# Opening of a macaron transformer block: statistics merge, low-part product and fill-in products rearranged

## The chip, the cores and the metric

The kernel runs on one core of one Trainium2 chip. The metric is device time in microseconds (us) of one execution; the median of the runs is given.

## What is computed

The input x is (4, 1024, 128) in float32. Three sub-layers follow each other: half of a mixture-of-experts feed-forward, an attention without softmax, and the same feed-forward again, each behind a layer norm and added to x. Cut to what matters here:

```python
def ffn(x):                                   # E = 16 experts, 2 shared units, F = 128
    scores = sigmoid(x @ router_w.T)          # group-limited top-4 of scores + bias
    combine = ...                             # (tokens, 16), 2.5 * normalised weights
    h = einsum('td,edf->etf', x, gate_w)
    u = einsum('td,edf->etf', x, up_w)
    y = einsum('etf,efd->etd', silu(h) * u, down_w)
    return einsum('etd,te->td', y, combine) + silu(x @ sh_gate_w) * (x @ sh_up_w) @ sh_down_w
x = x + 0.5 * ffn(layernorm(x))
x = x + attention(layernorm(x))
x = x + 0.5 * ffn(layernorm(x))
```

All 18 units (2 shared, 16 routed) are computed for every token; the combine weights are zero where an expert was not chosen.

## The kernel before

The 4096 tokens are eight blocks of 512. One **step** is one block through one feed-forward, so there are 16 steps, and a step has 18 **units** of 512 tokens each. A Python loop `pair(p, ...)` on every engine writes out two steps (36 units, `u` from 0 to 35, `w = u % 18`); only the first pair, where `first` is true, matters here, and its first step is the code's `early`. In the text, step 0, 1 and 2 are the first, second and third step, and unit u is that of step 0.

A float32 product is made of three products of rounded operands (`product`, L447): high weights by high activations (L449), low weights by high activations (L450), high weights by low activations (L451). A unit is nine such 128x512 products on TensorE: gate, up, and the down product of the unit four before it (`LAG = 4`). Around them:

- ScalarE: silu of the gate (L840), `A_hi`, the rounded product (L814), `W_hi`, the rounded weights (L718), copies of the transposed next block `XT` (L743) and its rounding `XT_hi` (L747), and the normalised next block `XN` (L733).
- VectorE: silu by combine weight `T` (L1137), that by up `A` (L1168), the routing of the next step in eight parts (`route`, L958 on), and the statistics of the step after: `bn_stats` (L938) and their merge (`merge_stats`, L899 to L912, called by `stats`).
- GpSimd: low parts, which are the difference of a value and its rounding: `W_lo` of the weights (L333), `A_lo` of the products (L340), `XT_lo` of the next block (`next_low`, L359), and the power -0.5 of the variance (L351).
- SyncE's queue issues every transfer.

Each engine's order is the order of the code; engines meet at semaphores. In step 0 the weights come in and are split while the first units run, so GpSimd has a `W_lo` beside most `A_lo` (table `SPLIT_AT`: units 4, 5 and 7 to 12).

Places that the change touches. At the start TensorE does 13 fill-in products (`keep_busy(WARM)`), a transpose, 2 fill-ins, four transposes of block 0 into the PSUM bank `prepP` (L480), the router logits (L488), and then `first_units` (L578 on), whose first gate product waits for `XT_lo` of step 0. The four transposes of `comb` at L569 (`spread`), behind the gate of unit 4, wait for the whole routing of step 0. PSUM bank `prepP` holds in turn the transposed block, the logits of the next step and the scratch tiles of `route`. The statistics of step 1 are merged in the prologue with one operand or the result of each instruction in PSUM (L1213 to L1227); those of step 2 are merged behind unit 13 by `merge_stats`, with all operands in SBUF. TensorE's gate of unit u waits for `T` of unit u - 2 (`gate_left`).

Of the kernel before, what the change touches and what calls it, by code (L numbers as in the profile page):

```python
# [28 lines left out]
F32 = mybir.dt.float32  # L29
F32R = mybir.dt.float32r  # L30
ALU = mybir.AluOpType
ACT = mybir.ActivationFunctionType
AX = mybir.AxisListType

P = 128
HEAD = 4
EPS = 1e-5
GROUPS, PER_GROUP = 4, 4
# [4 lines left out]
TILES = BLOCK // P  # L43
# [5 lines left out]
def macaron_kernel(nc, x, Wqkv_w, Wqkv_b, gn_w, gn_b, out_w, out_b, router_w, bias,  # L49
                   gate_w, up_w, down_w, sh_gate_w, sh_up_w, sh_down_w, out):  # L50
    BATCH, SEQ, D = x.shape
    E = router_w.shape[0]
# [14 lines left out]
    WARM, FILL = 13, 2  # L67
# [12 lines left out]
    with ctx:  # L80
# [15 lines left out]
        XT_hi = sb("XT_hi", [P, 2, BLOCK], F32R)  # L96
        XT_lo = sb("XT_lo", [P, 2, BLOCK], F32R)
# [8 lines left out]
        bst = sb("bst", [P, TILES, 6])  # L106
# [85 lines left out]
        prepP = pb("prepP")  # L192
# [136 lines left out]
        def _(pool):  # L329
# [61 lines left out]
            def pair(p, first, attention, last):  # L391
                n = PAIR * p
                for u in range(PAIR):
                    w, s = u % UNITS, u // UNITS
                    early = first and s == 0
                    if early and u in SPLIT_AT:
                        split_low(SPLIT_AT[u])
                    if first and u == 24:
                        pool.memset(XA[:, :, :], 1.0)
                    if w == 14 and not last:  # L400
                        step_rstd(2 * p + s + 2)
                    if w == (7 if early else 2) and not (last and s == 1):
                        next_low(2 * p + s + 1, (s + 1) % 2)
                    if attention and u == 4:

                        pool.wait_ge(att_seq, ATT_OPS * (p - ATT0) + 6)
                        pool.tensor_tensor(arstd[:, :], avar[:, :], half[:, :],
                                           ALU.pow).then_inc(att_pow, 1)
                        pool.wait_ge(att_pow, 3 * (p - ATT0) + 1)
                        pool.tensor_tensor(ashift[:, :], anmean[:, :], arstd[:, :],  # L410
                                           ALU.mult).then_inc(att_pow, 1)
                    if attention and u == 28:

                        pool.wait_ge(att_seq, ATT_OPS * (p - ATT0) + 17)
                        pool.tensor_tensor(grstd[:, :], gvar[:, :], half[:, 0:1],
                                           ALU.pow).then_inc(att_pow, 1)
                    if not (first and u == 0):
                        split_activations(n + u - 1, (u - 1) % SLOTS)
                    if attention and u in (33, 34):
                        g = u - 33  # L420
                        if g == 0:

                            pool.wait_ge(att_seq, ATT_OPS * (p - ATT0 + 1))
                        xb = X[:, bass.ds((p - ATT0) * BT + g * TILES, TILES), :]
                        pool.tensor_tensor(xb, xb, brow[:, :].unsqueeze(1).broadcast_to([P, TILES, P]),
                                           ALU.add).then_inc(row_added, 1)
# [17 lines left out]

        @block.tensor
        def _(pe):
            def product(dst, hi_w, lo_w, hi_x, lo_x, start, stop):  # L447

                pe.matmul(dst, hi_w, hi_x, start=start, stop=False)  # L449
                pe.matmul(dst, lo_w, hi_x, start=False, stop=False)  # L450
                return pe.matmul(dst, hi_w, lo_x, start=False, stop=stop)  # L451

            def down(n, u, t):
# [29 lines left out]
            def logits(t):  # L483

                pe.wait_ge(xt_ready, t + 1)
                bank = backP if isinstance(t, int) and t == 0 else prepP
                for j in range(TILES):
                    mm = pe.matmul(bank[:, j * E:(j + 1) * E], XT[:, j * P:(j + 1) * P], RT[:, :],  # L488
                                   start=True, stop=True)
                mm.then_inc(logits_done, 1)  # L490
# [87 lines left out]
            def first_units():  # L578

                def one(dst, u, i):  # L580
                    return product(dst[:, :], W_hi[:, u, i, :], W_lo[:, u, i, :], XT_hi[:, 0, :],
                                   XT_lo[:, 0, :], True, True)

                def gate(u):
                    pe.wait_ge(w_lo_done, u + 1)
                    if u == 0:
                        pe.wait_ge(xt_lo_ready, 1)
                    if u >= 2:
                        pe.wait_ge(silu_done, u - 1)
                    one(gateP[u % 2], u, 0).then_inc(gate_done, 1)  # L590

                def up(u):
                    one(first_up[u], u, 1).then_inc(up_done, 1)

                gate(0)
                up(0)
                gate(1)
                up(1)
                gate(2)
                gate(3)  # L600
                up(2)
                up(3)
                gate(4)
                pe.wait_ge(route_seq, ROUTE_OPS)
                spread(0)
                spread(1)
                transpose_weights(0)
                gate(5)

                pe.wait_ge(ct_ready, 1)  # L610
                up(4)
                pe.wait_ge(mul_done, 2)
                up(5)

                pe.wait_ge(gate_weighted, 1)
                spread(2)
                pe.wait_ge(mul_done, 3)
                spread(3)
                gate(6)

                pe.wait_ge(mul_done, 4)
                down(0, 0, 0)
                transpose_next(1)
                down(0, 1, 0)
# [65 lines left out]
            pe.transpose(attP[:, 3 * P:3 * P + E], R_in[:, :], ident[0:E, 0:E]).then_inc(setup_psum, 1)  # L690
            keep_busy(FILL)
            transpose_next(0)
            pe.wait_ge(setup_sb, 1)
            logits(0)
            pair(0, True, False, False)
# [202 lines left out]
        def _(dve):  # L898
# [37 lines left out]
            def rows(t, blk):  # L936
# [2 lines left out]
                                       .rearrange("p o d -> p (o d)"))  # L939
                ins.then_inc(stats_seq, 1)  # L940

            def stats(t):
                merge_stats(stats_seq, 4 * t, bst, nmean[:, :], vareps[:, :], parts)

# [10 lines left out]
            gscp = scratch(6, GROUPS)  # L955
            grank = prepP[:, TILES * (7 * E + GROUPS):TILES * (7 * E + 2 * GROUPS)]
            wsump = prepP[:, TILES * (7 * E + 2 * GROUPS):TILES * (7 * E + 2 * GROUPS + 1)]

            def route(t, part):
                base = ROUTE_OPS * t  # L960
# [1 line left out]
                selp4 = selp.rearrange("p t (g i) -> p (t g) i", i=PER_GROUP)  # L962
                if part == 0:
                    dve.wait_ge(logits_done, t + 1)
                    flat = (backP if isinstance(t, int) and t == 0 else prepP)[:, 0:TILES * E]

                    near_f = near[:, :, :].rearrange("p t e -> p (t e)")

# [171 lines left out]
            def pair(p, first, attention, last):  # L1140
                n, t0 = PAIR * p, 2 * p
                for u in range(PAIR):
# [27 lines left out]
                    if w == 13 and not (first and s == 0):  # L1170
                        residual(t0 + s - 1, 2 * ((p - 1 + s) % BATCH) + (1 - s))
                    if not (last and s == 1):
                        at = 6 if early else 0
                        if at + 2 <= w < at + 10:
                            route(t0 + s + 1, w - at - 2)
# [6 lines left out]
                        dve.wait_ge(mul_done, n + u + 1)  # L1182
                        rows(t0 + s + 2, 2 * ((p + 1) % BATCH) + s)
                    if w == (13 if early else 12) and not last:
                        stats(t0 + s + 2)
                    if first and u == PAIR - 1:
                        dve.tensor_scalar(blkm[:, :], blk1[:, :], 1.0 / HEAD, None,
                                          ALU.mult).then_inc(attended, 2)
# [98 lines left out]
```

## Time and profile before

| | |
|---|---|
| median of 3 runs | 670.13 us (669.88 to 670.77) |
| the profiled execution's own time | 671.6 us |
| its span, first to last instruction | 669.9 us |
| busy: TensorE, VectorE, GpSimd, ScalarE | 661.1, 522.3, 446.5, 406.4 us |
| mean granted clock of TensorE | 0.995 |

The profile lists instructions by line of the kernel, with out<-in by tile names. A timeline row is start, duration, engine, line, operation, operands, count, and in brackets how long the engine had been idle before it and what released it. TensorE rows overlap, since products are pipelined, so the distance of starts is the cost of one. The granted clock is 1.00 at 2.4 GHz and 0.50 at 1.2 GHz.

### The profile page before, as it was taken

How to read it: one execution, taken by the hardware profiler on the slowest of the kernel's cores; microseconds unless marked ns; L12 is line 12 of the kernel's file. 1: busy time of each engine (PE TensorE's matmuls, PEld its weight loads, DVE VectorE, ACT ScalarE, POOL GpSimd, SP SyncE). 2: the span in 40 equal slices, each digit the busy share in tenths (PEclk: the TensorE clock that was granted, in tenths of full speed). 3: DMA queues.
4: the chain of work that ended last, by engine and by line, in shares of the span. 5: the costliest groups of instructions: out<-in, count | busy, mean ns of one | idle time of the engine just before them, and what ended most of it. 6: DMA issues, size and time to landing. Idle time of an engine off the chain costs nothing.

```text
span 669.9 us, 10547 instructions
## 1 busy us (share of the span) xinstructions
PE 661.1 (99%) x3165; PEld 551.2 (82%) x3165; DVE 522.3 (78%) x1440; ACT 406.4 (61%) x817; POOL 446.5 (67%) x386
## 2 busy tenths in 40 slices
PE   7989999999999999999999999999999999999997
PEld 6868888888888888888888888888888888888886
DVE  6796969778687886878868778687795978868664
ACT  4856565565676556765657656676656565655554
POOL 6996666666756677666676666766667666666663
PEclk8999999999999999999999999999999999999999
DMA  9715170320506015060160510703306033150700
GB/s 232 264 58 201 54 252 2 139 114 27 226 2 234 20 45 211 0 221 33 26 229 1 199 55 17 252 1 134 136 12 259 0 131 139 46 225 0 270 0 32
DMA packets 30262, 75.38 MB, mean 113 GB/s; under 512 B 3569, under 2 KB 12545, under 8 KB 30209
## 3 DMA queue, kind: packets, MB, share of 16 engines
q1 hardware_dynamic: 30208, 74.74, 31.0%
q8 instruction: 25, 0.41, 0.2%
q14 instruction: 29, 0.23, 0.1%
HBM read 72.11 MB, written 2.62 MB: 112 GB/s over the span
## 4 chain that ended last, share of the span: by engine, by line
PE 96%; DVE 1%; DMA 1%; SPq 0%; POOL 0%; issue 0%; ACT 0%; DVEq 0%
PE gateP L449 10%; PE yP L451 10%; PE yP L449 10%; PE gateP L451 10%; PE gateP L450 10%; PE upP L451 10%; PE yP L450 10%; PE upP L449 10%; PE upP L450 10%; PE prepP L488 2%; PE attP L505 1%; PE backP L469 1%; PE prepP L480 1%; DMA W_in<-in_L_ffn_sh_down_w_dram 1%; PE attP L561 1%; PE backP L561 1%
## 5 line engine op out<-in xcount | busy, mean ns | idle before, releaser
L340 POOL TENSOR_TENSOR A_lo<-A,A_hi 128x512 fp32r<-128x512 f32 x287 | 370.6, 1293 | 205.2 <-ACT A_hi L814 205.2
L840 ACT ACTIVATE gateP<-gateP 128x512 f32<-128x512 f32 x252 | 146.6, 582 | 203.6 <-PE gateP L451 202.7
L1137 DVE TENSOR_TENSOR T<-gateP,CB 128x512 f32<-128x512 f32 x252 | 173.3, 688 | 89.1 <-ACT gateP L840 84.8
L814 ACT CAST A_hi<-A 128x512 fp32r<-128x512 f32 x287 | 176.0, 613 | 12.4 <-DVE A L1168 9.5
L1168 DVE TENSOR_TENSOR A<-upP,T 128x512 f32<-128x512 f32 x254 | 175.6, 691 | 8.7
L449 PE MATMUL gateP<-XT_hi,W_hi 128*128 128x512 f32 x288 | 119.1, 414 | 2.1 <-DVE T L1137 1.7
L449 PE MATMUL yP<-A_hi,W_hi 128*128 128x512 f32 x288 | 113.5, 394 | 0.0
L451 PE MATMUL yP<-A_lo,W_hi 128*128 128x512 f32 x288 | 112.9, 392 | 0.0
L451 PE MATMUL gateP<-XT_lo,W_hi 128*128 128x512 f32 x288 | 112.8, 392 | 0.0
L450 PE MATMUL gateP<-XT_hi,W_lo 128*128 128x512 f32 x288 | 112.7, 391 | 0.0
L450 PE MATMUL yP<-A_hi,W_lo 128*128 128x512 f32 x288 | 112.3, 390 | 0.0
L451 PE MATMUL upP<-XT_lo,W_hi 128*128 128x512 f32 (+1 forms) x286 | 112.1, 392 | 0.0
L449 PE MATMUL upP<-XT_hi,W_hi 128*128 128x512 f32 (+1 forms) x286 | 112.1, 392 | 0.0
L450 PE MATMUL upP<-XT_hi,W_lo 128*128 128x512 f32 (+1 forms) x286 | 111.8, 391 | 0.0
L449 PEld LDWEIGHTS yP<-A_hi,W_hi 128*128 128x128 f32 x288 | 54.2, 188 | 13.2 <-POOL A_lo L340 1.9
L451 PEld LDWEIGHTS gateP<-XT_lo,W_hi 128*128 128x128 f32 x288 | 54.3, 189 | 11.8
L449 PEld LDWEIGHTS gateP<-XT_hi,W_hi 128*128 128x128 f32 x288 | 54.7, 190 | 11.2 <-issue 2.1
L451 PEld LDWEIGHTS yP<-A_lo,W_hi 128*128 128x128 f32 x288 | 54.2, 188 | 11.7
L451 PEld LDWEIGHTS upP<-XT_lo,W_hi 128*128 128x128 f32 x286 | 54.1, 189 | 11.7
L450 PEld LDWEIGHTS upP<-XT_hi,W_lo 128*128 128x128 f32 x286 | 54.0, 189 | 11.6
L449 PEld LDWEIGHTS upP<-XT_hi,W_hi 128*128 128x128 f32 x286 | 53.9, 188 | 11.7
L450 PEld LDWEIGHTS yP<-A_hi,W_lo 128*128 128x128 f32 x288 | 54.2, 188 | 11.0
(223 smaller groups left out, 647.0 us busy)
## 6 DMA issues: line engine op xcount, KB each, us to landing
CB<-combT SPq DMA_DIRECT2D x126, 512.0 KB, 6.9
out_dram<-X SPq DMA_DIRECT2D x7, 256.0 KB, 2.0
X<-in_L_attn_x_dram SPq DMA_DIRECT2D x3, 512.0 KB, 9.8
W_in<-in_L_ffn_gate_w_dram SPq DMA_DIRECT2D x4, 256.0 KB, 5.2
W_in<-in_L_ffn_up_w_dram SPq DMA_DIRECT2D x4, 256.0 KB, 5.3
W_in<-in_L_ffn_down_w_dram SPq DMA_DIRECT2D x4, 256.0 KB, 5.4
X<-in_L_attn_x_dram SPq DMA_DIRECT2D x2, 256.0 KB, 3.1
combT<-CT SPq DMA_DIRECT2D x16, 32.0 KB, 1.8
```

The source lines that it names most:

```text
L340: pool.tensor_tensor(A_lo[:, slot, :], A[:, slot, :], A_hi[:, slot, :].bitcast(F32), ALU.subtract).then_inc(low_done, 1)
L449: pe.matmul(dst, hi_w, hi_x, start=start, stop=False)
L450: pe.matmul(dst, lo_w, hi_x, start=False, stop=False)
L451: return pe.matmul(dst, hi_w, lo_x, start=False, stop=stop)
L469: mm = pe.transpose(backP[:, j * P:(j + 1) * P], YT[:, j * P:(j + 1) * P], ident[:, :])
L480: mm = pe.transpose(prepP[:, j * P:(j + 1) * P], XN[:, j, :], ident[:, :])
L488: mm = pe.matmul(bank[:, j * E:(j + 1) * E], XT[:, j * P:(j + 1) * P], RT[:, :], start=True, stop=True)
L561: mm = pe.matmul(bank[:, j * P:(j + 1) * P], XAT[:, g * TILES + j, :], Bm[:, :], start=True, stop=True)
L814: act.copy(A_hi[:, v % SLOTS, :], A[:, v % SLOTS, :]).then_inc(high_done, 1)
L840: act.activation(dst, gateP[u % 2][:, :], ACT.Silu).then_inc(silu_done, 1)
L1137: dve.tensor_tensor(T[:, u % TS, :], silu, weights, ALU.mult).then_inc(gate_weighted, 1)
L1168: dve.tensor_tensor(A[:, u % SLOTS, :], bank[:, :], gated, ALU.mult).then_inc(mul_done, 1)
```

## The change

Four edits, all in the first step or ahead of it:

1. `stats_in_psum` merges the statistics of step 2, behind unit 13 of step 0, in seven instructions, each with an operand or the result in PSUM (free columns of `prepP`), in place of the seven of `merge_stats`.
2. `XT_lo` of step 1 is made on VectorE out of `prepP` behind unit 7, and no longer on GpSimd out of `XT`. So that `prepP` still holds the block, the logits of step 1 go to the bank `backP`.
3. The first gate product of the kernel waits for `XT_hi`, and only its third product for `XT_lo`.
4. Two more fill-in products (`keep_busy(FILL)`) stand between the transposes of block 0 and its logits.

```diff
-                    if w == (7 if early else 2) and not (last and s == 1):
+                    if w == 2 and not early and not (last and s == 1):
                         next_low(2 * p + s + 1, (s + 1) % 2)
...
-            def product(dst, hi_w, lo_w, hi_x, lo_x, start, stop):
+            def product(dst, hi_w, lo_w, hi_x, lo_x, start, stop, low_of_step_0=False):
 
                 pe.matmul(dst, hi_w, hi_x, start=start, stop=False)
                 pe.matmul(dst, lo_w, hi_x, start=False, stop=False)
+                if low_of_step_0:
+                    pe.wait_ge(xt_lo_ready, 1)
                 return pe.matmul(dst, hi_w, lo_x, start=False, stop=stop)
...
-                bank = backP if isinstance(t, int) and t == 0 else prepP
+                bank = backP if isinstance(t, int) and t < 2 else prepP
...
-                        pe.wait_ge(xt_lo_ready, 1)
+                        pe.wait_ge(xt_hi_ready, 1)
...
             transpose_next(0)
+            keep_busy(FILL)
             pe.wait_ge(setup_sb, 1)
             logits(0)
...
+            def stats_in_psum(t, bank, count):
+
+                base = 4 * t
+                sums = bank[:, 0:2 * TILES].rearrange("p (j c) -> p j c", c=2)
+                diffp, within = bank[:, 2 * TILES:3 * TILES], bank[:, 3 * TILES:4 * TILES]
+                both = bst[:, :, :].rearrange("p j (h c) -> p j c h", h=2)[:, :, 1:3, :]
+                dve.wait_ge(stats_seq, base + 1)
+                dve.tensor_reduce(sums, both, AX.X, ALU.add).then_inc(stats_seq, 1)
+                dve.wait_ge(stats_seq, base + 2)
+                for dst in (parts[:, 0, :], diffp):
+                    dve.scalar_tensor_tensor(dst, bst[:, :, 1], 2.0, sums[:, :, 0], ALU.mult, ALU.subtract)
+                dve.tensor_scalar(nmean[:, :], sums[:, :, 0], -0.5, None, ALU.mult)
+                dve.tensor_scalar(within, sums[:, :, 1], 1.0 / P, EPS, ALU.mult, ALU.add).then_inc(stats_seq, 1)
+                dve.wait_ge(stats_seq, base + 3)
+                dve.scalar_tensor_tensor(parts[:, 1, :], parts[:, 0, :], 0.25, diffp, ALU.mult,
+                                         ALU.mult).then_inc(spread_square, 1)
+                dve.wait_ge(spread_square, count)
+                dve.tensor_tensor(vareps[:, :], parts[:, 1, :], within, ALU.add).then_inc(stats_seq, 1)
...
+                        if early and u == 7:
+
+                            dve.wait_ge(xt_hi_ready, 2)
+                            dve.tensor_tensor(XT_lo[:, 1, :], prepP[:, :], XT_hi[:, 1, :].bitcast(F32),
+                                              ALU.subtract).then_inc(xt_lo_ready, 1)
...
-                        stats(t0 + s + 2)
+                        if early:
+                            stats_in_psum(2, prepP[:, FREE_AT:FREE_AT + 4 * TILES], 2)
+                        else:
+                            stats(t0 + s + 2)
```

TensorE's queue at the start, with the semaphores that a row waits for, before:

```order
L480 MATMUL prepP<-ident,XN 128x128 x3
L488 MATMUL backP<-RT,XT 128x16 [waits xt_ready,setup_sb]
L488 MATMUL backP<-RT,XT 128x16 x3
L449 MATMUL gateP<-XT_hi,W_hi 128x512 [waits xt_lo_ready,w_lo_done]
L450 MATMUL gateP<-XT_hi,W_lo 128x512
L451 MATMUL gateP<-XT_lo,W_hi 128x512
```

and now:

```order
L482 MATMUL prepP<-ident,XN 128x128 x3
L578 MATMUL yP<-ones 128x128 x2
L490 MATMUL backP<-RT,XT 128x16 [waits xt_ready,setup_sb]
L490 MATMUL backP<-RT,XT 128x16 x3
L449 MATMUL gateP<-XT_hi,W_hi 128x512 [waits xt_hi_ready,w_lo_done]
L450 MATMUL gateP<-XT_hi,W_lo 128x512
L453 MATMUL gateP<-XT_lo,W_hi 128x512 [waits xt_lo_ready]
```

Two fill-ins stand between the transposes and the logits, and the wait for `XT_lo` has moved two products back.

GpSimd's queue in units 5 to 8 of step 0, before:

```order
L340 TENSOR_TENSOR A_lo<-A,A_hi 128x512 x2
L333 TENSOR_TENSOR W_lo<-W_in,W_hi 128x384
L359 TENSOR_TENSOR XT_lo<-XT,XT_hi 128x512
L340 TENSOR_TENSOR A_lo<-A,A_hi 128x512
L333 TENSOR_TENSOR W_lo<-W_in,W_hi 128x384
```

and VectorE's in units 7 and 8 now (L1160 is `T`, L1191 is `A`, L992 the first instruction of `route` for step 1):

```order
L1160 TENSOR_TENSOR T<-gateP,CB 128x512
L1191 TENSOR_TENSOR A<-upP,T 128x512
L1199 TENSOR_TENSOR XT_lo<-prepP,XT_hi 128x512
L1160 TENSOR_TENSOR T<-gateP,CB 128x512
L1191 TENSOR_TENSOR A<-upP,T 128x512
L992 TENSOR_SCALAR near<-backP 128x64
```

The L359 row is gone from GpSimd's queue in this step, and L1199 stands in VectorE's between `A` of unit 7 and `T` of unit 8.

VectorE's queue behind unit 13 of step 0, before:

```order
L1031 MAX top<-masked 128x8 x4
L903 TENSOR_TENSOR parts<-bst 128x4
L904 TENSOR_TENSOR parts<-bst 128x4
L905 TENSOR_TENSOR parts<-bst 128x4
L907 TENSOR_SCALAR nmean<-parts 128x4
L908 SCALAR_TENSOR_TENSOR parts<-parts 128x4
L909 TENSOR_SCALAR parts<-parts 128x4
L912 TENSOR_TENSOR vareps<-parts 128x4
L1137 TENSOR_TENSOR T<-gateP,CB 128x512
```

and now:

```order
L1054 MAX top<-masked 128x8 x4
L952 TENSOR_REDUCE prepP<-bst 128x8
L955 SCALAR_TENSOR_TENSOR parts<-bst,prepP 128x4
L955 SCALAR_TENSOR_TENSOR prepP<-bst,prepP 128x4
L956 TENSOR_SCALAR nmean<-prepP 128x4
L957 TENSOR_SCALAR prepP<-prepP 128x4
L959 SCALAR_TENSOR_TENSOR parts<-parts,prepP 128x4
L962 TENSOR_TENSOR vareps<-parts,prepP 128x4
L1160 TENSOR_TENSOR T<-gateP,CB 128x512
```

The place and the count of the seven are the same; none has only SBUF operands any more.

## Rows read from the trace of the kernel before

**Rows 1.** The page: TensorE's busy time, and the chain that ended last by engine.

```profile
PE 661.1 (99%) x3165; PEld 551.2 (82%) x3165; DVE 522.3 (78%) x1440; ACT 406.4 (61%) x817; POOL 446.5 (67%) x386
...
PE 96%; DVE 1%; DMA 1%; SPq 0%; POOL 0%; issue 0%; ACT 0%; DVEq 0%
```

**Rows 2.** Windows: busy us by engine, then TensorE's granted clock, DMA share, GB/s.

```profile
10.00:15.00 5.00, 4.66 (x16) 3.66 (x16) 4.48 (x23) 2.72 (x7) 3.65 (x5) 0.66 1.20 292
...
50.00:55.00 5.00, 5.00 (x20) 3.94 (x19) 4.42 (x11) 3.57 (x9) 3.56 (x4) 0.75 0.02 3
```

**Rows 3.** Timeline of TensorE, end of step 0 (start, duration, idle before and releaser).

```profile
36.85 0.46 PE L449 MATMUL yP<-A_hi,W_hi 128*128 128x512 f32 x1
...
45.73 0.50 PE L449 MATMUL yP<-A_hi,W_hi 128*128 128x512 f32 x1
...
46.30 0.39 PE L451 MATMUL yP<-A_lo,W_hi 128*128 128x512 f32 x1
48.41 0.47 PE L449 MATMUL gateP<-XT_hi,W_hi 128*128 128x512 f32 x1 [1.73 <-DVE T L1137]
...
52.60 0.39 PE L451 MATMUL gateP<-XT_lo,W_hi 128*128 128x512 f32 x1
```

**Rows 4.** Timeline of VectorE, units 13 to 15 of step 0.

```profile
43.52 3.42 DVE L903 TENSOR_TENSOR parts<-bst 128x4 f32<-128x4 f32 x1
...
47.58 0.69 DVE L1137 TENSOR_TENSOR T<-gateP,CB 128x512 f32<-128x512 f32 x1
...
49.51 0.68 DVE L1137 TENSOR_TENSOR T<-gateP,CB 128x512 f32<-128x512 f32 x1
```

**Rows 5.** Timeline of GpSimd in step 0.

```profile
31.95 1.33 POOL L359 TENSOR_TENSOR XT_lo<-XT,XT_hi 128x512 fp32r<-128x512 f32 x1
...
41.13 1.07 POOL L333 TENSOR_TENSOR W_lo<-W_in,W_hi 128x384 fp32r<-128x384 f32 x1
...
43.35 1.06 POOL L333 TENSOR_TENSOR W_lo<-W_in,W_hi 128x384 fp32r<-128x384 f32 x1
44.33 2.59 POOL L340 TENSOR_TENSOR A_lo<-A,A_hi 128x512 fp32r<-128x512 f32 x2
47.71 1.01 POOL L351 TENSOR_TENSOR rstd<-vareps,half 128x4 f32<-128x4 f32 x1 [0.80 <-DVE vareps L912]
```

**Rows 6.** Groups of instructions, by form: L903 in the whole kernel (count | busy, mean ns).

```profile
L903 DVE TENSOR_TENSOR parts<-bst 128x4 f32<-128x4 f32 x15 | 7.7, 514 | 0.0
```

**Rows 7.** Timeline of TensorE from the start to the first weights' spread.

```profile
6.44 0.71 PE L576 MATMUL yP<-ones 128*128 128x128 f32 x4
...
9.21 1.03 PE L488 MATMUL backP<-RT,XT 128*128 128x16 f32 x8 [0.88 <-DVE XT L1221]
10.59 0.47 PE L449 MATMUL gateP<-XT_hi,W_hi 128*128 128x512 f32 x1 [0.34 <-POOL W_lo L333]
...
11.57 0.61 PE L450 MATMUL upP<-XT_hi,W_lo 128*128 128x512 f32 x1
...
14.97 0.41 PE L449 MATMUL gateP<-XT_hi,W_hi 128*128 128x512 f32 x1
...
18.43 0.60 PE L569 MATMUL backP<-ident,comb 128*128 128x128 f32 x4
```

**Rows 8.** Timeline of VectorE and GpSimd in the same stretch.

```profile
8.61 1.95 POOL L333 TENSOR_TENSOR W_lo<-W_in,W_hi 128x384 fp32r<-128x384 f32 x2 [2.16 <-ACT W_hi L718]
...
8.98 0.15 DVE L1224 SCALAR_TENSOR_TENSOR parts<-parts,attP 128x4 f32<-128x4 f32 x1
...
9.16 0.16 DVE L1227 TENSOR_TENSOR vareps<-parts,attP 128x4 f32<-128x4 f32 x1
...
9.75 0.69 DVE L1230 TENSOR_TENSOR XT_lo<-prepP,XT_hi 128x512 fp32r<-128x512 f32 x1 [0.43 <-ACT XT_hi L747]
...
16.86 0.28 DVE L1049 SCALAR_TENSOR_TENSOR comb<-prepP,wrec 128x64 f32<-128x64 f32 x1
```

**Rows 9.** Timeline of VectorE, units 7 and 8 of step 0.

```profile
28.85 0.69 DVE L1168 TENSOR_TENSOR A<-upP,T 128x512 f32<-128x512 f32 x1
30.83 0.69 DVE L1137 TENSOR_TENSOR T<-gateP,CB 128x512 f32<-128x512 f32 x1 [1.29 <-ACT gateP L840]
```

**Rows 10.** The chain that ended last, near the kernel's end: one unit apart.

```profile
656.64 0.23 PE gateP L449
...
658.68 0.23 PE gateP L449
```

More of the change, by code:

```diff
@@ L581, in one @@
                     return product(dst[:, :], W_hi[:, u, i, :], W_lo[:, u, i, :], XT_hi[:, 0, :],
-                                   XT_lo[:, 0, :], True, True)
+                                   XT_lo[:, 0, :], True, True, u == 0 and i == 0)
                 def gate(u):
@@ L957, in _ @@
             wsump = prepP[:, TILES * (7 * E + 2 * GROUPS):TILES * (7 * E + 2 * GROUPS + 1)]
+            FREE_AT = TILES * (7 * E + 2 * GROUPS + 1)
             def route(t, part):
@@ L964, in route @@
                     dve.wait_ge(logits_done, t + 1)
-                    flat = (backP if isinstance(t, int) and t == 0 else prepP)[:, 0:TILES * E]
+                    flat = (backP if isinstance(t, int) and t < 2 else prepP)[:, 0:TILES * E]
                     near_f = near[:, :, :].rearrange("p t e -> p (t e)")
```

## Prediction, made before the changed kernel was run

> **What bounds the kernel now.** The page first. TensorE is busy 661.1 of 669.9 us, and the chain that ended last lies on it for 96% [rows 1]. So time can only be won where TensorE stands idle or runs at a lower clock. The windows tell where: the granted clock is 1.00 everywhere but in two stretches of the first 55 us, 0.66 over 10 to 15 us and 0.75 over 50 to 55 us [rows 2]. All four edits act there. In full flow a unit (nine products) costs 658.68 - 656.64 = 2.04 us, 0.227 each [rows 10].
>
> Then the timeline at the end of step 0. TensorE ends a down product at 46.30 + 0.23 = 46.53 and starts the gate of unit 16 at 48.41, released by `T` of unit 14 [rows 3]: 1.88 us idle. VectorE reached that `T` late, since L903, a 128x4 addition, took 3.42 us [rows 4]; over the kernel it is 7.7 us in 15, so the other 14 average 0.31 [rows 6]. During those 3.42 us GpSimd ran a `W_lo` and two `A_lo` back to back and ended them at 44.33 + 2.59 = 46.92; L903 ended at 46.94. GpSimd then idled 0.80 us, waiting for the statistics [rows 5]. I read this as a hold: L903 has both inputs in SBUF, and it went ahead when GpSimd ran out of work. The seven instructions of the prologue's merge that touch PSUM show no such hold: L1224 and L1227 took 0.15 and 0.16 us inside a GpSimd `W_lo` pair of 8.61 to 10.56 [rows 8].
>
> After the idle stretch TensorE's clock fell to 1.2 GHz: from 48.41 to 52.60 it started 11 products in 4.19 us, where 11 at 0.227 are 2.50.
>
> **The change part by part.**
>
> *Merge in PSUM.* Seven instructions become seven; by L1224 and L1227 each is about 0.16 us [rows 8], with one semaphore step more, under 0.1 us. The hold of 3.42 - 0.17 = 3.25 us goes. What is late next? `T` of unit 14 moves from 47.58 to 44.33, is done at 45.02 and seen by TensorE about 0.14 later (48.41 - 48.27), while TensorE wants it at 46.53: 1.4 us to spare. So the whole wait goes, 1.88 us, and with it what made the clock fall, 4.19 - 2.50 = 1.69 us. Bounds: none of it, if the hold has another cause; 3.57 us in all.
>
> Here the trace and the Trainium skill differ. The row shows a hold over three GpSimd instructions. The page SBUF — State Buffer, section "SBUF: two separate sides", says that a VectorE instruction with two SBUF inputs and a GpSimd one share a port pair as an exclusive lock, held for one instruction, the other being blocked meanwhile. By that rule L903 would have waited only to the end of the `W_lo`, about 0.9 us, and the other 2.4 us would have a cause that this edit may not touch. I go by the row, whose end coincides with GpSimd's last instruction within 0.02 us; the rule's reading is rival D.
>
> *XT_lo from GpSimd to VectorE.* GpSimd loses one instruction of 1.33 us (about 1.25 from start to start) [rows 5]. It matters, because in units 8 to 12 GpSimd sets TensorE's pace: `W_lo` comes every 43.35 - 41.13 = 2.22 us [rows 5], and the down products from 36.85 to 45.73 come every 8.88 / 4 = 2.22 us [rows 3], against 2.04 to 2.05. Four units by 0.17 are 0.7 us. With 1.25 us in hand GpSimd stays ahead of TensorE over those units. Gain 0.7 us; bounds 0 and 0.7. VectorE gets 0.69 us more, by the same operation on the same shapes in the prologue [rows 8]. `XT_hi` is long ready then (ScalarE makes it in unit 6), and VectorE idled 1.29 us between `A` of unit 7 and `T` of unit 8 [rows 9]: hidden. If that cover were gone, it would use up 0.69 of VectorE's spare time further on. The logits in another bank cost the same.
>
> *First gate earlier.* TensorE ends the logits at 10.24 and starts the first gate at 10.59 [rows 7]. The profile names a `W_lo` as the releaser, but the first `W_lo` was done by 9.6 and the second at 10.56, too late for a 10.55 weight load; `XT_lo` ended at 9.75 + 0.69 = 10.44 [rows 8], 0.15 before. Now two products start at 10.25, and the third at 10.7 finds `XT_lo` ready. Gain 0.34 us. Nothing else on TensorE waits behind it.
>
> *Two fill-ins.* They cost about 0.45 us at 2.4 GHz (the pair at 6.44 took 0.52 of weight loads, 0.71 with its tail [rows 7]) and lie in the 0.88 us in which TensorE waits for `XT`: hidden, 0. If `XT` came earlier, they would cost up to 0.45. What they may change is the clock. Today TensorE is half idle from 8.3 to 10.6, and from 11.57 the products come every 0.43 us: eight from 11.57 to 14.97 in 3.40 us [rows 7], against 1.82 at full clock, 1.58 lost. Ahead of the second fall it had idled 1.88 us. After the edits the stretch before 11.57 has 0.88 - 0.45 + 0 in place of 0.88 + 0.34 us of idle time. No row tells whether that is enough; I take it as slightly likelier than not, because the idle time falls to a third. If the clock stays up, not all of 1.58 + 0.34 is won: nine products of units 0 to 4 by 0.69 from 10.25 end at 16.5, and the transposes behind them wait for the routing, which VectorE ends at 16.86 + 0.28 = 17.14 whatever TensorE does [rows 8]. They start at 17.3 in place of 18.43 [rows 7]: 1.13 us in all.
>
> **The sum**, with the clock up in the opening: 1.13 + 0.7 + 1.88 + 1.69 = 5.4 us. Later stretches are TensorE-bound in any case and only shift. The check on what is late next: with everything 1.13 earlier and the hold gone, `T` of unit 14 is at 47.58 - 4.38 = 43.20, seen at 44.03; TensorE wants it at 46.53 - 1.13 - 0.70 = 44.70. `T` of unit 15 is at 49.51 - 4.38 = 45.13 [rows 4], seen at 45.96, wanted at 44.70 + 2.05 = 46.75. So VectorE has 0.7 us to spare: enough, but no more. The profiled execution would go from 671.6 (span 669.9 and 1.7 around it) to 666.2. The median of the runs lies 1.5 below its own time; against it the same gain gives 670.13 - 5.4 = 664.7.
>
> **The rivals.**
>
> *A, the forecast (0.46):* as above, 664.7.
>
> *B, the fill-ins don't hold the clock in the opening (0.32).* The logits are eight short passes of 16 columns and may leave TensorE nearly as idle as before. Then the opening wins 0.34 only: 0.34 + 0.7 + 1.88 + 1.69 = 4.6, 665.5.
>
> *C, a new wait takes part of it back (0.10).* VectorE's 0.7 us to spare is used up by the added 0.69 us, or TensorE's new pause before the transposes, 16.5 to 17.3, costs a stretch of low clock. One stretch was worth 1.58 to 1.69 us: 666.3 to 667.2.
>
> *D, the hold is not of the port, or only 0.9 of it (0.07).* Then L903's successors stay slow, TensorE's wait and the second fall stay; only opening and pace are won, 1.8 or 1.0 us: 668.3 to 669.1. For it: one long row among 15. Against it: the coincidence of the two ends.
>
> *E, the other side (0.05): VectorE's new `XT_lo` is itself held by GpSimd.* It starts at about 29.5, when GpSimd has some three rounds of 2.22 us before it (units 12 to 14 of `W_lo`, and the `A_lo` between them), so it would be held till about 36.6. `T` of unit 8 would come at 37.3 in place of 30.83; VectorE has no idle time from there to the end of the step, so everything behind is 6.5 late, less the 3.25 of the old hold: the first gate of step 1 is about 1.3 later than now, 671.5. It decides once the hold is longer than about 5.5 us. Against it: L1230, the same instruction from PSUM, took 0.69 us while GpSimd ran a `W_lo` [rows 8].
>
> **How the numbers follow.** A difference under 0.2% (1.3 us) can't be told from none here. A, B and C are faster by more, as is most of D: 0.93. The rest of D and a fifth of E are within 0.2%: 0.03. E otherwise is slower: 0.04. The range takes in A and B with their bounds and most of C: from 664.0 (A and 0.7 more, if small waits of units 1 to 5 go as well) to 667.0; it leaves out D, E and the end of C, about 0.15.
>
> **What would show it.** L952 to L962 each about 0.16 us, with no row of microseconds among them; no wait of TensorE near 45 us, and a clock of 1.00 from 45 to 55 us; down products of units 8 to 11 every 2.05 us; GpSimd with gaps in units 8 to 13; the first gate at 10.25. For A against B: the granted clock from 10 to 15 us, and a pause of about 0.75 us before the transposes of `comb`. The prediction is wrong if a small VectorE instruction still takes over 1 us behind unit 13, if L1199 takes more than 0.8 us, or if TensorE waits for VectorE anywhere in units 8 to 17.

## Result and profile after

| | before | after |
|---|---|---|
| median | 670.13 us | 665.96 us |
| lowest to highest of 5 | 668.60 to 671.51 | 665.81 to 666.03 |
| profiled execution: own time, span | 671.6, 669.9 | 665.98, 664.2 |
| granted clock, mean | 0.995 | 1.000 |

Three of before's five times are the three given ahead; the profiled execution is none of the five.

The ratio is 0.9937, with a 95% interval of 0.9924 to 0.9951. The median fell by 4.2 us and the two traces differ by 5.7 us of span. Why these two are not the same number is what the forecast had wrong, and it is taken up below. The times of after also spread over 0.2 us only, those of before over 2.9.

The windows of after, in the columns of [rows 2]: no stretch has a lowered clock.

```profile
10.00:15.00 5.00, 5.00 (x24) 3.93 (x24) 4.48 (x21) 3.66 (x9) 4.69 (x7) 1.00 1.19 293
...
50.00:55.00 5.00, 5.00 (x28) 4.24 (x27) 1.68 (x3) 3.22 (x6) 3.98 (x4) 1.00 0.36 98
```

VectorE's timeline of after behind unit 13, the place of [rows 4]:

```profile
42.01 0.41 DVE L1054 MAX8 top<-masked 128x8 f32<-128x20 f32 x4
42.34 0.16 DVE L952 TENSOR_REDUCE prepP<-bst 128x8 f32<-128x16 f32 x1
...
43.14 0.16 DVE L962 TENSOR_TENSOR vareps<-parts,prepP 128x4 f32<-128x4 f32 x1
43.25 0.69 DVE L1160 TENSOR_TENSOR T<-gateP,CB 128x512 f32<-128x512 f32 x1
...
45.17 0.68 DVE L1160 TENSOR_TENSOR T<-gateP,CB 128x512 f32<-128x512 f32 x1
```

The seven instructions take 0.16 us each and 0.96 in all, where the one L903 took 3.42 and the seven of before 4.11 (43.52 to 47.63). `T` of unit 14 is at 43.25 (43.20 was worked out ahead) and that of unit 15 at 45.17 (45.13). GpSimd was busy meanwhile; it ran two `A_lo` back to back right through the merge:

```profile
40.40 1.02 POOL L333 TENSOR_TENSOR W_lo<-W_in,W_hi 128x384 fp32r<-128x384 f32 x1
41.38 2.54 POOL L340 TENSOR_TENSOR A_lo<-A,A_hi 128x512 fp32r<-128x512 f32 x2
43.87 1.01 POOL L351 TENSOR_TENSOR rstd<-vareps,half 128x4 f32<-128x4 f32 x1
```

TensorE's timeline of after, the places of [rows 3] and [rows 7]:

```profile
37.72 0.39 PE L449 MATMUL yP<-A_hi,W_hi 128*128 128x512 f32 x1
39.76 0.39 PE L449 MATMUL yP<-A_hi,W_hi 128*128 128x512 f32 x1
41.80 0.39 PE L449 MATMUL yP<-A_hi,W_hi 128*128 128x512 f32 x1
43.84 0.39 PE L449 MATMUL yP<-A_hi,W_hi 128*128 128x512 f32 x1
```

```profile
9.37 1.04 PE L490 MATMUL backP<-RT,XT 128*128 128x16 f32 x8 [0.43 <-DVE XT L1252]
10.25 0.48 PE L449 MATMUL gateP<-XT_hi,W_hi 128*128 128x512 f32 x1
...
16.02 0.39 PE L449 MATMUL gateP<-XT_hi,W_hi 128*128 128x512 f32 x1
...
17.34 0.65 PE L571 MATMUL backP<-ident,comb 128*128 128x128 f32 x4 [0.48 <-DVE comb L1072]
```

Down products come every 2.04 us in place of 2.22, and from unit 5 to the end of step 0 no product waits for VectorE. In the opening the first gate is at 10.25, the gate of unit 4 at 16.02, and TensorE then waits 0.48 us for the routing. A pause there was forecast, of about 0.75 us.

The added `XT_lo` on VectorE takes 0.68 us in what was idle time; 0.57 of that is left in front of `T` of unit 8:

```profile
28.41 0.68 DVE L1199 TENSOR_TENSOR XT_lo<-prepP,XT_hi 128x512 fp32r<-128x512 f32 x1
29.66 0.69 DVE L1160 TENSOR_TENSOR T<-gateP,CB 128x512 f32<-128x512 f32 x1 [0.57 <-ACT gateP L843]
```

**Where the time went.** Two marks in each trace divide it: the start of the transposes of `comb` (end of the opening) and the start of the transposes of block 2 (end of step 0). From the second mark to the end it is 615.5 to 615.6 us in every trace of the table: 669.9 - 54.34 before, 664.2 - 48.72 after. So all of the difference lies in step 0. The table is from TensorE's timelines and is used throughout; its kernels are those of the experiments below:

| kernel | opening, to the first mark | first to second mark | span |
|---|---|---|---|
| before | 18.43 | 35.91 | 669.9 |
| only the merge | 18.86 | 32.51 | 666.9 |
| only `XT_lo` | 18.71 | 33.28 | 667.6 |
| only the fill-ins | 17.11 | 34.12 | 666.8 |
| only the earlier gate | 17.14 | 33.88 | 666.6 |
| merge and fill-ins | 17.29 | 32.13 | 665.0 |
| without the merge | 17.78 | 32.62 | 665.9 |
| without `XT_lo` | 17.13 | 32.00 | 664.7 |
| without the fill-ins | 17.19 | 31.39 | 664.1 |
| without the earlier gate | 17.66 | 31.39 | 664.5 |
| after | 17.34 | 31.38 | 664.2 |

### The profile page after: what moved, and what is told of

It is laid out like the page before. It is cut to its first block, busy times and chain, and to the rows that moved or that the text cites. A ratio compares the mean times of both kernels' runs of the same rounds, so it can differ in the third digit from the quotient of the medians.

```text
span 664.2 us, 10555 instructions
## 1 busy us (share of the span) xinstructions
PE 658.0 (99%) x3169; PEld 550.7 (83%) x3169; DVE 519.2 (78%) x1441; ACT 406.4 (61%) x817; POOL 445.1 (67%) x385
## 4 chain that ended last, share of the span: by engine, by line
PE 98%; DVE 1%; issue 0%; ACT 0%; POOL 0%; DVEq 0%; POOLq 0%
PE gateP L449 10%; PE yP L453 10%; PE yP L449 10%; PE yP L450 10%; PE upP L449 10%; PE gateP L453 10%; PE upP L453 10%; PE gateP L450 10%; PE upP L450 10%; PE prepP L490 2%; PE attP L507 1%; PE prepP L482 1%; PE backP L471 1%; PE yP L578 1%; PE backP L563 1%; PE attP L563 1%
## 5 line engine op out<-in xcount | busy, mean ns | idle before, releaser
L1160 DVE TENSOR_TENSOR T<-gateP,CB 128x512 f32<-128x512 f32 x252 | 173.2, 687 | 88.5 <-ACT gateP L843 80.7
L1191 DVE TENSOR_TENSOR A<-upP,T 128x512 f32<-128x512 f32 x254 | 175.6, 691 | 8.7
```

The source lines that it names most:

```text
L1160: dve.tensor_tensor(T[:, u % TS, :], silu, weights, ALU.mult).then_inc(gate_weighted, 1)
L1191: dve.tensor_tensor(A[:, u % SLOTS, :], bank[:, :], gated, ALU.mult).then_inc(mul_done, 1)
```

## Experiments

The first four make one edit of the change alone in the kernel before, the next four take one out of the changed kernel. Each was timed beside the kernel before, in 5 to 12 executions.

Besides its time, the mean granted clock of every one of these executions is known, and it tells how many falls the execution had, a fall being a stretch at 1.2 GHz in the first 60 us. In the trace of before each fall takes 1.7 us off the clock, (1 - 0.66) x 5 in the opening and (1 - 0.91) x 5 + (1 - 0.75) x 5 over 45 to 55 us, which is 0.0025 of the span of 669.9. So two falls read 0.995, one reads 0.997 (0.996 in the trace of only `XT_lo`, which has one), and none 1.000 or 0.999 (the trace at 0.999, of the second probe below, has its only low stretch behind TensorE's last product). Counted this way, with the probes left out:

| kernel | no fall | one | two |
|---|---|---|---|
| before (in four comparisons) | 8 (668.50 to 668.82) | 34 (669.91 to 670.89) | 1 (671.67) |
| only the merge | 3 (666.57 to 666.73) | 3 (668.21 to 668.80) | |
| only `XT_lo` | 5 (667.37 to 667.52) | 2 (669.01, 669.27) | |
| only the fill-ins | 9 (668.54 to 669.32) | 3 (669.94 to 670.05) | |
| only the earlier gate | 5 (668.26 to 668.65) | 7 (669.73 to 670.21) | |
| without the fill-ins | 2 (665.82, 665.83) | 3 (667.17 to 667.33) | |
| after; without the merge, without `XT_lo`, without the earlier gate; merge and fill-ins; fewer fill-ins | 30 | | |

### Only the merge in PSUM

```diff
-                        stats(t0 + s + 2)
+                        if early:
+                            stats_in_psum(2, prepP[:, FREE_AT:FREE_AT + 4 * TILES], 2)
+                        else:
+                            stats(t0 + s + 2)
```

Expected: 

> The kernel before with the merge of step 2 in PSUM and nothing else. Hold theory (the SBUF-only addition L903 waits for GpSimd): no small VectorE row over 0.2 us behind unit 13, no wait of TensorE near 47 us, no clock of 1.2 GHz behind it, GpSimd still pacing units 8 to 12; the span 3.6 us under that of before (669.9 to 666.3), the clock from 10 to 15 us still 0.66. Rival (the hold has another cause, or GpSimd's shorter queue is what cures it): within 1 us of before.

Measured: 667.47 us (666.57 to 668.80 in 6), ratio 0.9961 (0.9946 to 0.9977). These are two groups: 666.57 to 666.73 with a clock of 1.000 and 668.21 to 668.80 with 0.997. The profiled execution (668.66, span 666.9) is of the second group. It has no wait of TensorE behind the opening, a clock of 1.00 from 45 to 55 us and 0.66 from 10 to 15 us. Its merge starts with the first of these rows, while GpSimd runs the other two:

```profile
43.97 0.16 DVE L951 TENSOR_REDUCE prepP<-bst 128x8 f32<-128x16 f32 x1
```

```profile
43.84 1.00 POOL L333 TENSOR_TENSOR W_lo<-W_in,W_hi 128x384 fp32r<-128x384 f32 x1
44.81 2.54 POOL L340 TENSOR_TENSOR A_lo<-A,A_hi 128x512 fp32r<-128x512 f32 x2
```

The merge alone takes away the hold, the wait and the second fall: first to second mark 35.91 to 32.51, 3.4 us, where 3.57 was worked out. GpSimd's queue is untouched here and ran without a gap through the merge, so it is not its relief that does it. The span came out 0.6 above the 666.3 expected: 0.43 of that is a later first mark (18.86 for 18.43), since the fill-ins at the start took 5.89 us in place of 4.58, and the rest is the 0.17 that the merge gave less.

### Only XT_lo on VectorE

```diff
-                    if w == (7 if early else 2) and not (last and s == 1):
+                    if w == 2 and not early and not (last and s == 1):
                         next_low(2 * p + s + 1, (s + 1) % 2)
...
-                bank = backP if isinstance(t, int) and t == 0 else prepP
+                bank = backP if isinstance(t, int) and t < 2 else prepP
...
+                        if early and u == 7:
+                            dve.wait_ge(xt_hi_ready, 2)
+                            dve.tensor_tensor(XT_lo[:, 1, :], prepP[:, :], XT_hi[:, 1, :].bitcast(F32),
+                                              ALU.subtract).then_inc(xt_lo_ready, 1)
```

Expected: 

> The kernel before with XT_lo of step 1 on VectorE (and the logits of step 1 in the other bank) and nothing else. Hold theory: L903 is still held until GpSimd runs dry, which comes 1.25 us earlier: about 2.1 us in place of 3.42; TensorE's wait shrinks from 1.7 to about 0.5 us, the pace of 2.22 us per unit goes to 2.05 (0.7 us): 2 us gained, 3.6 if the clock then stays up. Rival (only the pace is won): 0.7 us gained, L903 as long as before.

Measured: 667.44 us (667.37 to 669.27 in 7), ratio 0.9966 (0.9954 to 0.9977); five of the seven lie from 667.37 to 667.52 and two, with a clock of 0.997 and 0.996, at 669.01 and 669.27. VectorE's, GpSimd's and TensorE's timelines of the profiled execution, which is the one at 669.27:

```profile
43.80 2.18 DVE L905 TENSOR_TENSOR parts<-bst 128x4 f32<-128x4 f32 x1
```

```profile
42.43 1.03 POOL L333 TENSOR_TENSOR W_lo<-W_in,W_hi 128x384 fp32r<-128x384 f32 x1
43.41 2.55 POOL L340 TENSOR_TENSOR A_lo<-A,A_hi 128x512 fp32r<-128x512 f32 x2
46.75 1.01 POOL L351 TENSOR_TENSOR rstd<-vareps,half 128x4 f32<-128x4 f32 x1 [0.80 <-DVE vareps L914]
```

```profile
47.45 0.47 PE L449 MATMUL gateP<-XT_hi,W_hi 128*128 128x512 f32 x1 [1.32 <-DVE T L1159]
```

The hold is 2.18 us, as expected (2.1), and ends at 45.98 with GpSimd's run (45.96). Both theories missed TensorE's side: its wait is 1.32 us, not 0.5. The reason is that TensorE, no longer paced by GpSimd, comes to the same place 0.7 us earlier: of the 1.24 us that the hold is shorter, only 0.5 can shorten the wait, and it went from 1.73 to 1.32. The shorter hold and the better pace are not a sum. The clock is 1.00 from 45 to 55 us here, so this wait was not followed by a fall; the fall is in the opening (0.66). The first-to-second-mark time is 33.28, 0.6 to 0.8 under the kernels that have the whole wait and no second fall (34.12 and 33.88, next two).

### Only the two fill-ins

```diff
             transpose_next(0)
+            keep_busy(FILL)
```

Expected: 

> The kernel before with the two added fill-ins and nothing else. Fill-in theory: granted clock 1.00 from 10 to 15 us, the transposes behind the gate of unit 4 at 17.3 in place of 18.43: span 1.1 us shorter. Rival (the earlier first gate is what keeps the clock up): clock 0.66 from 10 to 15 us, no change of time.

Measured: 668.66 us (668.54 to 670.05 in 12), ratio 0.9987 (0.9978 to 0.9997). Its windows and timelines:

```profile
10.00:15.00 5.00, 4.66 (x22) 3.85 (x22) 4.48 (x23) 3.73 (x9) 4.38 (x7) 1.00 1.16 305
45.00:50.00 5.00, 3.31 (x15) 2.70 (x15) 4.76 (x23) 2.66 (x6) 4.00 (x6) 1.00 0.01 3
```

```profile
46.69 0.47 PE L449 MATMUL gateP<-XT_hi,W_hi 128*128 128x512 f32 x1 [1.71 <-DVE T L1160]
```

The opening is as expected: the clock stays up, the transposes start at 17.11. But something unexpected stands beside it. TensorE waited 1.71 us for VectorE, as good as the 1.73 of before, and this time the clock did not fall behind it. The fall does not follow every such stretch. Three of the twelve executions had one fall (0.997); where in them it lies was not traced.

### Only the earlier first gate

```diff
-                        pe.wait_ge(xt_lo_ready, 1)
+                        pe.wait_ge(xt_hi_ready, 1)
```

(and the wait for `xt_lo_ready` ahead of the third product)

Expected: 

> The kernel before with the first gate product waiting for XT_hi and nothing else. Fill-in theory: first gate product at 10.25 in place of 10.59, clock still falls in the opening, 0.3 us gained, less than can be told. Rival (this edit keeps the clock up): clock 1.00 from 10 to 15 us, 1.1 us gained.

Measured: 669.81 us (668.26 to 670.21 in 12), ratio 0.9991 (0.9981 to 1.0002): no difference that can be told in the median. The profiled execution is one of the five near 668.4 (its own time is 668.31), its first gate is at 10.05, and it has no fall at all, although TensorE waited 1.72 us for VectorE:

```profile
10.00:15.00 5.00, 5.00 (x23) 3.80 (x23) 4.48 (x23) 3.80 (x9) 4.92 (x7) 1.00 1.18 300
45.00:50.00 5.00, 3.51 (x15) 2.69 (x15) 4.72 (x25) 2.87 (x7) 4.00 (x5) 1.00 0.02 3
```

By its trace alone this would have passed for the edit that keeps the clock up. Its twelve times say otherwise: five lie from 668.26 to 668.65 and seven from 669.73 to 670.21, and nothing between. The times of the kernel before fall apart in the same way. Of 24 executions in this comparison six lie from 668.51 to 668.82, none from there to 669.91, and the other 18 from 669.91 to 671.67. The granted clock says what parts them: 1.000 for the six, 0.996 or 0.997 for 17 of the others, and 0.995 for the one at 671.67. With the fill-ins alone it is eight from 668.54 to 669.00, one at 669.32 and three from 669.94 to 670.05.

### Without the merge in PSUM

The changed kernel with `stats(t0 + s + 2)` back in place of `stats_in_psum`.

Expected: 

> The changed kernel with the old SBUF-only merge of step 2. Hold theory: the first instruction of the merge starts at 42.3 us and is held until GpSimd's run ends at 43.9, so about 1.6 us; VectorE has 0.7 us to spare, so TensorE waits about 0.7 us: 666.7, or 668.3 if the clock falls after it. Rival (GpSimd's relief alone cures the hold): no row over 0.4 us, 666.0 as the changed kernel.

Measured: 667.25 us (667.08 to 667.76), 1.3 us above the changed kernel. VectorE's, GpSimd's and TensorE's timelines:

```profile
42.79 1.59 DVE L906 TENSOR_TENSOR parts<-bst 128x4 f32<-128x4 f32 x1
```

```profile
41.82 2.55 POOL L340 TENSOR_TENSOR A_lo<-A,A_hi 128x512 fp32r<-128x512 f32 x2
45.16 1.01 POOL L351 TENSOR_TENSOR rstd<-vareps,half 128x4 f32<-128x4 f32 x1 [0.79 <-DVE vareps L915]
```

```profile
45.86 0.47 PE L449 MATMUL gateP<-XT_hi,W_hi 128*128 128x512 f32 x1 [0.74 <-DVE T L1160]
```

Hold 1.59 and wait 0.74, where 1.6 and 0.7 were expected; the hold ends at 44.38, GpSimd's run at 44.37. The first-to-second-mark time is 32.62 against 31.38, 1.24 more. Of that, 0.89 is the idle stretch itself, from the end of the last product before it (start 44.74 and 0.23) to 45.86; the other 0.35 lies in the products behind it and was not followed. The clock did not fall in this execution or in the other four.

### Without XT_lo on VectorE

The changed kernel with `XT_lo` of step 1 back on GpSimd.

Expected: 

> The changed kernel with XT_lo of step 1 back on GpSimd. Theory: GpSimd paces the down products of units 8 to 11 at 2.22 us in place of 2.05; 0.3 to 0.7 us slower than the changed kernel, no fall of the clock. Rival (the pace was set by something else): no difference from 665.96.

Measured: 666.50 us (666.17 to 666.72), 0.5 above; first to second mark 32.00, 0.62 above. TensorE's down products:

```profile
37.51 0.39 PE L449 MATMUL yP<-A_hi,W_hi 128*128 128x512 f32 x1
39.55 0.41 PE L449 MATMUL yP<-A_hi,W_hi 128*128 128x512 f32 x1
41.68 0.50 PE L449 MATMUL yP<-A_hi,W_hi 128*128 128x512 f32 x1
43.91 0.50 PE L449 MATMUL yP<-A_hi,W_hi 128*128 128x512 f32 x1
```

They come every 2.04 us at first, then 2.13 and 2.23: GpSimd sets the pace again, only later than before, probably since its queue is ahead from the opening on.

### Without the fill-ins

Expected: 

> The changed kernel without the two added fill-ins. Fill-in theory: the clock falls in the opening as before (0.66 over 10 to 15 us), 0.8 to 1.1 us slower than the changed kernel: 666.8 to 667.1. Rival (the earlier first gate was enough): 665.96 and clock 1.00.

Measured: 667.17 us, and again in two groups: 665.82 and 665.83, and 667.17, 667.31 and 667.33. Neither theory as written holds: without the fill-ins the clock falls in some executions and not in others. The granted clock is 1.000 in the lower two and 0.997, one fall, in the upper three. The profile was taken of one at 665.82, so that this fall lies in the opening wasn't seen in a trace. What supports it is that no long wait is left elsewhere, and the distance of 1.3 to 1.5 us: in traces with the fall the opening lasts 18.43 (before), 18.86 (only the merge) and 18.71 us (only `XT_lo`), in those without it and with the same late first gate 17.11 and 17.29, so 1.1 to 1.8 us less.

### Without the earlier first gate

Expected: 

> The changed kernel with the first gate product waiting for XT_lo again. Theory: the first gate starts 0.3 us later, but TensorE's pause before the transposes, which wait for the routing, shrinks by as much: no difference from 665.96. Rival (the routing is not what is waited for, or the clock falls for lack of those 0.3 us): 0.3 to 1.5 us slower.

Measured: 666.18 us (665.95 to 666.26), 0.2 above the changed kernel; the two ranges overlap by 0.08. In its profiled execution `XT_hi` came late (9.61 in place of 9.26), so `XT_lo` and all of the routing behind it on VectorE came 0.3 later and the first gate was at 11.09, 0.84 later than after. Yet the span is only 0.3 longer: the transposes wait for the routing in either case. So the edit is worth 0 to 0.2 us, which can't be told from nothing.

### Merge and fill-ins together

The kernel before with these two edits.

Expected: 

> The kernel before with the merge in PSUM and the two added fill-ins, without the move of XT_lo and the earlier first gate. If the terms add up: 0.7 us (the pace of GpSimd) above the changed kernel, 666.6, in executions in which the clock stays up, and nearly all executions are of that kind. Rival (the earlier first gate is needed too for a steady clock): a second group of executions about 1.4 us higher, as in the kernel before.

Measured: 666.73 us (666.60 to 667.17), ratio 0.9950 (0.9937 to 0.9964): one group, 0.8 above the changed kernel. So these two edits give 3.4 of the 4.2 us, the move of `XT_lo` most of the rest, and the earlier gate isn't needed for a steady clock. All five have a clock of 0.999 or 1.000.

### A probe: how long is such an addition held?

```diff
+                    if early and u == 9:
+                        dve.tensor_tensor(probe[:, :], bst[:, :, 1], bst[:, :, 4], ALU.add)
```

The changed kernel, with an addition of the same two 128x4 operands as L903, behind `A` of unit 9, where GpSimd has much work before it. Nobody reads `probe`. In the second kernel the last operand is `rcl[:, :, 0]`, which lies in PSUM.

Expected, two SBUF operands: 

> The changed kernel with one more VectorE instruction, a 128x4 addition of two SBUF operands into a tile that nobody reads, behind A of unit 9 of step 0, while GpSimd runs low parts back to back. Reading from the trace of before: it is held until GpSimd's queue has nothing to run, over several GpSimd instructions, 2 us or more. The rule of one instruction: it is held to the end of the GpSimd instruction then running, under 1.3 us. No hold by GpSimd at all: 0.17 us.

Expected, one operand in PSUM: 

> The same added addition at the same place, with its second operand in PSUM. Hold by the second SBUF operand: 0.17 us here, and the time of the changed kernel. If the place or the added instruction were at fault: as long as with two SBUF operands.

Measured, one time each: 672.71 us and 666.66 us. The second is 0.7 above the changed kernel's median, which the 0.15 us of the addition don't explain; in that execution the 13 fill-ins at the start took 5.92 us, and the first mark came at 17.87 in place of 17.34, which makes up 0.53 of it. VectorE's and GpSimd's timelines of the first:

```profile
33.15 5.83 DVE L1195 TENSOR_TENSOR probe<-bst 128x4 f32<-128x4 f32 x1
```

```profile
32.32 1.28 POOL L341 TENSOR_TENSOR A_lo<-A,A_hi 128x512 fp32r<-128x512 f32 x1
33.57 1.01 POOL L334 TENSOR_TENSOR W_lo<-W_in,W_hi 128x384 fp32r<-128x384 f32 x1
...
37.98 0.98 POOL L334 TENSOR_TENSOR W_lo<-W_in,W_hi 128x384 fp32r<-128x384 f32 x1
41.56 1.28 POOL L341 TENSOR_TENSOR A_lo<-A,A_hi 128x512 fp32r<-128x512 f32 x1 [2.61 <-ACT A_hi L818]
```

and VectorE's of the second:

```profile
33.86 0.15 DVE L1195 TENSOR_TENSOR probe<-bst,prepP 128x4 f32<-128x4 f32 x1
```

The addition was held for 5.83 us, over the GpSimd instruction then running and five whole ones behind it, and went ahead at 38.96, when GpSimd had nothing more to run, since VectorE itself no longer fed it. TensorE waited 3.88 us for it, and its clock then fell: 0.50 over 40 to 45 us and 0.90 over 45 to 50. Wait and fall together cover the 6.8 us by which this kernel is above the changed one. With one operand in PSUM the addition took 0.15 us in the same place, inside a GpSimd `A_lo` of 32.99 to 34.27.

Each probe is one execution, but the hold was seen in six traces, and every time the held row ended within 0.03 us of the end of GpSimd's run: 3.42 us (before), 3.08 (only the fill-ins), 2.85 (only the earlier gate), 2.18 (only `XT_lo`), 1.59 (without the merge) and 5.83. The trace of before has the small form of it too. L903 runs 15 times there. The one that met an idle GpSimd, at 4.41, took 0.17 us; the 13 of later steps took 0.24 to 0.37 and each ended 0.02 to 0.03 us behind an `A_lo` that had no instruction queued behind it. One of these pairs:

```profile
83.70 0.29 DVE L903 TENSOR_TENSOR parts<-bst 128x4 f32<-128x4 f32 x1
```

```profile
82.68 1.28 POOL L340 TENSOR_TENSOR A_lo<-A,A_hi 128x512 fp32r<-128x512 f32 x1 [0.74 <-ACT A_hi L814]
```

So a 128x4 addition of two SBUF operands is held, the same addition with one operand in PSUM is not, and the hold lasts until GpSimd's run of instructions ends.

### Fewer fill-ins at the start

```diff
-    WARM, FILL = 13, 2
+    WARM, FILL = 10, 2
```

Expected: 

> The changed kernel with 10 fill-ins at the start in place of 13. In the profiles so far the 13 took 4.55 to 5.92 us, depending on when the clock rose, and where they took over 5.3 the transposes of block 0, and the routing behind them, came up to 0.6 us later. Theory: 10 end by 6.1 us even at 1.2 GHz, the transposes always start by 7.7, and the routing ends by 17.2: 665.6 to 665.9, up to 0.3 us better than the changed kernel. Rival: with fewer fill-ins the clock is still low or falls in the opening in some executions: single executions 0.5 to 1.5 us above 666.0.

Measured: 665.85 us (665.70 to 666.03), against 665.96 (665.81 to 666.03): inside each other, no gain that can be told. The transposes of block 0 started at 7.67 in place of 7.89 and the routing was done at 17.11 in place of 17.28, which TensorE waits for. It is no worse, and its profile shows the theory's mechanism at the size of 0.17 us; whether it ever pays more in executions in which the fill-ins run slowly for longer stays open. The rival is not borne out: no execution lies above 666.03, and all five have a clock of 0.999 or 1.000.

## Why the prediction was right, and where it was off

Right in its mechanism at nearly every step of the trace, and off in one step, from trace to median. The range held. The point did not do as well: 665.96 is 1.3 above the forecast of 664.7 and nearer to rival B's 665.5 and to C's 666.3, and the mechanisms of neither (the clock still falls in the opening, a new wait) happened. The number alone would not have chosen A; the traces do. That the range took the result in owes something to its upper end, which had been set for B and C.

*The hold and the merge.* As worked out: no hold, `T` of unit 14 at 43.25, no wait, no fall. Merge alone gave 3.4 us in the trace for 3.57.

*One instruction or all of GpSimd's run.* Here the prediction went by the row and against the rule of the Trainium skill (SBUF — State Buffer, "SBUF: two separate sides"), by which the lock is held for one instruction. The case agrees with the page that two SBUF inputs are what brings the conflict (5.83 us against 0.15), and not with the length: the probe was held over six instructions. Rival D, which rested on that rule, falls. Rival E falls too, with L1199 at 0.68 us while GpSimd ran two `A_lo` from 26.75 to 29.29. Of rival C nothing showed: no wait for VectorE in units 5 to 17, and a clock of 1.00 after the pause in front of the transposes.

*XT_lo.* 0.6 to 0.75 us in the traces for 0.7 (32.13 to 31.38, 32.00 to 31.38), and hidden on VectorE. Two things about it the forecast did not say. Alone it also cuts the hold by 1.24 us, and TensorE gains 0.4 of that. And it does not act where the forecast placed all four edits, in the two stretches of lowered clock: the pace of 2.22 us is that of a stretch with a clock of 1.00, in which the window of before counts TensorE as fully busy (the first column behind the window's length):

```profile
40.00:45.00 5.00, 5.00 (x23) 3.63 (x22) 4.90 (x15) 2.23 (x5) 5.00 (x5) 1.00 0.00 0
```

Busy time and clock together don't show here that TensorE is paced; the distance of starts does.

*Opening.* Case A of the two: 18.43 to 17.34 is 1.09 us for 1.13. The chances given to A and B treated this as yes or no. The runs show a third thing: with the old opening the fall comes in some executions and not in others. Among the kernels in which no wait of over 0.8 us follows, a fall came in 6 of 11 executions without the added fill-ins (only the merge, without the fill-ins) and in none of 30 with them; in the one of the six that was traced it lies in the opening. So the fill-ins do keep the clock up. The three executions with a fall of the fill-ins alone had the 1.7 us wait behind unit 13 as well, and may have fallen there.

*The sum.* For the profiled execution 671.6 was to become 666.2; it became 665.98. The step that failed is the next one, "against it the same gain gives 670.13 - 5.4". Its sum takes off two falls, 1.69 behind the wait and, within the 1.13, the one of the opening, as if every execution had both. The profiled execution of before had both. The granted clock of the others says that this is rare: one of 43 had two falls, 34 had one, and 8 had none. The median execution lost one fall's worth: 670.1 against 668.6 for those without a fall, 1.5 us. Taking the wait (1.88) and the pace (0.7) from 668.6 as well gives 666.0, which is the median measured: 4.1 us in place of 5.4, where 4.17 was measured. Which of the two falls the 34 had is not shown, as none of them was traced.

The sign was there to be read: the profiled execution's own time stood 1.5 us above the median, against 0.0 after the change, and I treated that as a constant.

## What to carry to other kernels

A VectorE instruction with two SBUF operands, here a 128x4 addition, can stand for as long as GpSimd runs without a pause (1.6 to 5.8 us in six traces); look for rows that are far longer than their group's others and end with a GpSimd run, and give them an operand in PSUM, or thin out GpSimd's queue there. Where a profiled execution lies above the median of the runs, what it shows of the clock is not what the median execution loses: count such falls by the clock and the groups of the times, not by one trace. And edits that meet at the same wait, a shorter hold and a faster pace here, don't simply add up.

## What the runs showed of the hardware that I had not expected

- A held VectorE instruction is passed over by GpSimd instruction after instruction: six in the probe, 5.83 us. It does not get its turn between two.
- The same idle stretch of TensorE, 1.7 us at the same place, was followed by a fall to 1.2 GHz in the trace of before (0.75 over 50 to 55 us) and by none in two other kernels (1.00 over 45 to 55 us). Waits of 1.32 and 0.74 us were followed by none, one of 3.88 us by a fall; each of these is one trace.
- The 13 fill-ins at the start took 4.58 us in the trace of before and 5.48 in that of after, the same instructions from the same start at 1.77. They are 26 passes on TensorE. A pass starts every 0.21 us until 4.7 us in the trace of before and until 6.6 us in that of after, and every 0.11 us behind. I take the change as the clock's rise from 1.2 to 2.4 GHz, by the factor of two; the windows don't show it, since their clock column reads 1.00 on both sides of it.

```profile
1.77 5.48 PE L578 MATMUL yP<-ones 128*128 128x128 f32 x26 [1.77 <-POOL ident L367]
```

- With the opening filled and the wait gone, the spread went as well: 2.9 us before, 0.2 after.
